# The output product of a decoder layer's last block as a three-term f32r split instead of fp32

## The reference

```
q, k, v = x @ Wq, x @ Wk, x @ Wv                    # heads split
attn = softmax(k . q / sqrt(256)) over the last axis # "bkq"
z = (attn @ v) with heads merged                     # 4096 tokens x 256
z = l2_normalize(z @ Wo)
z = l2_normalize(z @ Wff)
z = gelu(z)                                          # exact gelu
out = layernorm(x + z)
```

## Time and profile before

| | us |
|---|---|
| median of 3 runs | 1932.04 (1929.75 to 1933.5) |
| the profiled execution | 1932.61 |
| its span (first to last instruction) | 1930.8 |
| output stage in it, 1853.3 to the end | 77.5 |

### The profile page before, as it was taken

The page is one execution under the profiler, slowest core; times in us unless marked ns, Lnnn a source line. Parts: engine busy times, 40 slices in busy tenths (PEclk is TensorE's granted clock), DMA queues, the critical chain, the costliest instruction groups (busy, mean ns, idle before and its releaser), DMA issues. The chain is left out here.

```text
span 1930.8 us, 45100 instructions
## 1 busy us (share of the span) xinstructions
PE 1802.6 (93%) x16198; PEld 1200.4 (62%) x16198; DVE 1458.1 (76%) x2707; ACT 1509.4 (78%) x4429; POOL 670.7 (35%) x778
## 2 busy tenths in 40 slices
PE   6999999999999999779999988899999999999995
PEld 5888888888888888648999987722222222222232
DVE  7677777777777777535666665599999999989956
ACT  6777777777777777437898865599999999989964
POOL 2343344433333344303766640022222222222222
PEclk9999999999999999989999998999999999999998
DMA  7233332233323322152101006733453344335002
GB/s 175 45 62 61 61 61 61 62 60 58 63 57 63 62 59 54 23 157 60 33 25 44 18 4 145 232 45 45 63 70 45 52 65 61 45 49 80 6 19 69
DMA packets 139782, 121.74 MB, mean 63 GB/s; under 512 B 78875, under 2 KB 111535, under 8 KB 139567
## 3 DMA queue, kind: packets, MB, share of 16 engines
q1 hardware_dynamic: 139567, 118.88, 31.3%
HBM read 77.29 MB, written 41.53 MB: 62 GB/s over the span
## 5 line engine op out<-in xcount | busy, mean ns | idle before, releaser
L1918 DVE TENSOR_REDUCE s_neg_max<-s_ring 128x1 f32<-128x1024 f32 x512 | 580.7, 1211 | 24.4 <-PE s_ring L1832 24.2
L1880 ACT ACTIVATE s_prob<-s_ring,s_neg_max 128x1024 f32<-128x1024 f32 x512 | 570.5, 1115 | 14.7 <-DVE s_neg_max L1918 14.6
L1845 PE MATMUL s_acc<-s_prob,s_v_norm 128*32 128x256 f32 x4096 | 327.9, 393 | 11.9 <-ACT f_zT_all L1872 9.8
L1832 PE MATMUL s_ring<-f_stack 128*128 128x512 bf16 x1024 | 312.6, 388 | 11.6 <-ACT s_prob L1880 7.0
L1901 POOL TENSOR_TENSOR s_row_inv<-s_row_sum,s_neg_one 128x4 f32<-128x4 f32 x128 | 128.9, 1007 | 411.8 <-ACT s_prob L1880 411.8
L492 ACT ACTIVATE a_prob<-a_psum,a_neg_max 128x128 f32<-128x128 f32 x512 | 179.8, 377 | 60.6 <-DVE a_neg_max L691 60.6
L1845 PEld LDWEIGHTS s_acc<-s_prob,s_v_norm 128*32 128x32 f32 x4096 | 81.5, 108 | 229.7 <-issue 213.3
L586 POOL TENSOR_SCALAR a_relu_ring<-a_qT 128x512 f32<-128x512 f32 x64 | 98.7, 1558 | 343.1 <-ACT a_qT L463 315.8
L1832 PEld LDWEIGHTS s_ring<-f_stack 128*128 128x128 bf16 x1024 | 58.4, 97 | 235.5 <-ACT s_prob L1880 216.2
L731 DVE SCALAR_TENSOR_TENSOR a_att<-a_psum,a_keep_cols,a_num_s 128x128 f32<-128x128 f32 x256 | 72.1, 344 | 132.7 <-ACT a_num_s L514 132.7
L1271 ACT ACTIVATE x_prob<-x_psum,x_neg_max 128x77 f32<-128x77 f32 x512 | 160.8, 337 | 14.2 <-DVE x_neg_max L1428 14.1
(11 more groups left out here) (197 smaller groups left out, 4043.2 us busy)
## 6 DMA issues: line engine op xcount, KB each, us to landing
f_stack<-qk_thirds SPq DMA_DIRECT2D x256, 128.0 KB, 6.0
segment_values<-a_v_stage SPq DMA_DIRECT2D x64, 256.0 KB, 3.5
a_v_pos<-segment_values SPq DMA_DIRECT2D x512, 32.0 KB
qk_thirds<-p_third SPq DMA_DIRECT2D x16, 768.0 KB, 8.0
a_x_in<-in_x_dram SPq DMA_DIRECT2D x16, 256.0 KB, 3.3
a_x_res<-in_x_dram SPq DMA_DIRECT2D x32, 128.0 KB, 2.9
after_attention<-a_normed SPq DMA_DIRECT2D x32, 128.0 KB, 2.4
x_x_in<-after_attention SPq DMA_DIRECT2D x32, 128.0 KB, 2.1
```

Source lines behind the costliest of these rows:

```text
L1832: last = pe.matmul(ring[n % 3][:, f * HALF:(f + 1) * HALF], k_stack[:, slot, j, kt * P:(kt + 1) * P], q_stack[:, slot, j, f * HALF:(f + 1) ...
L1845: last = pe.matmul(acc[32 * j:32 * j + 32, s], v_norm[:, step // KT % 2, step % 4, j, :], prob[:, step % 4, j, s], start=step % (2 * KT) = ...
L1880: act.activation(prob[:, step % 4, j, :], ring[n % 3][:, :], ACT.Exp, bias=neg_max[:, step % 2, j:j + 1], accum_out=row_sum[:, step % 4, j ...
L1918: dve.tensor_reduce(neg_max[:, step % 2, j:j + 1], ring[n % 3][:, :], AX_X, ALU.max, negate=True).then_inc(max_ready, 1)
```

## The change

The product z @ [Wo | Wo Wff] is made from f32r parts by the same `split_matmuls` as the projections. `w_both` becomes `w_split`, a high and a low f32r tensor. Wo is loaded into a tensor of its own, `w_out`; its high part is copied by ScalarE after batch 0 of the thirds and its low part subtracted by GpSimd. Of the folded half the high part is ScalarE's old copy, the low part a new subtraction on VectorE behind it. In the output stage `high(n)` on ScalarE copies a step's z (128x1024 values) to f32r and `low(n)` on VectorE subtracts it from z; both are made two steps ahead, at the head of each iteration, into rings of three slots. TensorE waits for both and issues six f32r matmuls of 512 columns per tile instead of two fp32 ones. GpSimd's order in the output stage is unchanged.

```diff
@@ -1550,10 +1550,10 @@
         stack_landed = [ctx.enter_context(nc.semaphore(f"f_stack{n}_landed")) for n in range(2)]
-        w_both = sb("w_both", [P, ZC, 2 * D])
-        emit_thirds(nc, x2_all, wq, wk, wv, wo, wff, parts, v_all, w_both, stacks, stack_landed, B, S)
+        w_split = [sb(f"w_{part}", [P, ZC, 2 * D], F32R) for part in ("hi", "lo")]
+        emit_thirds(nc, x2_all, wq, wk, wv, wo, wff, parts, v_all, w_split, stacks, stack_landed, B, S)
         zT_all = sb("zT_all", [P, B, ZC, S])
         emit_key_softmax(nc, parts, v_all, stacks, stack_landed, zT_all, B, S)
-        emit_gelu_output(nc, x2_all, zT_all, w_both, out, B, S)
+        emit_gelu_output(nc, x2_all, zT_all, w_split, out, B, S)
 
 
-def emit_thirds(nc, x2_all, wq, wk, wv, wo, wff, parts, v_all, w_both, stacks, stack_landed, B, S):
+def emit_thirds(nc, x2_all, wq, wk, wv, wo, wff, parts, v_all, w_split, stacks, stack_landed, B, S):
 
@@ -1589,2 +1589,4 @@
             sem("both_taken"))
+        wo_high, wo_low, both_low = sem("wo_high"), sem("wo_low"), sem("both_low")
+        w_out = sb("w_out", [P, ZC, D])
         woT = W[0][:, :, :].rearrange("p a b -> p (a b)")
@@ -1607,3 +1609,3 @@
                     at = 32 * j + half * HD
-                    sp.dma_start(w_both[at:at + HD, :, 0:D],
+                    sp.dma_start(w_out[at:at + HD, :, :],
                                  wo.rearrange("(c r h i) n -> r h i c n", c=ZC, r=2, h=4)[half, j]
@@ -1675,3 +1677,3 @@
                         at = (c * ZC + g) * P
-                        last = pe.transpose(wide[0][:, at:at + P], w_both[:, g, c * P:(c + 1) * P], ident[:, :])
+                        last = pe.transpose(wide[0][:, at:at + P], w_out[:, g, c * P:(c + 1) * P], ident[:, :])
                 last.then_inc(wo_turned, 1)
@@ -1725,4 +1727,7 @@
                          ).then_inc(high_done, 1)
-            for b in range(B):
-                batch(b, b % 2, b == 0, b == B - 1)
+            batch(0, 0, True, False)
+            act.wait_ge(wo_landed, 16 * 8)
+            act.copy(w_split[0][:, :, 0:D], w_out[:, :, :]).then_inc(wo_high, 1)
+            for b in range(1, B):
+                batch(b, b % 2, False, b == B - 1)
             act.wait_ge(wo_turned, 1)
@@ -1730,3 +1735,3 @@
             act.wait_ge(both_done, 1)
-            act.copy(w_both[:, :, D:2 * D], wide[1][:, 0:ZC * D].rearrange("p (g n) -> p g n", g=ZC)
+            act.copy(w_split[0][:, :, D:2 * D], wide[1][:, 0:ZC * D].rearrange("p (g n) -> p g n", g=ZC)
                      ).then_inc(both_taken, 1)
@@ -1739,2 +1744,5 @@
                                pattern=[[-1, P]], channel_multiplier=1).then_inc(c_ident, 1)
+            pool.wait_ge(wo_high, 1)
+            pool.tensor_tensor(w_split[1][:, :, 0:D], w_out[:, :, :], w_split[0][:, :, 0:D].bitcast(F32), ALU.subtract
+                               ).then_inc(wo_low, 1)
 
@@ -1777,2 +1785,5 @@
                 batch(b, b % 2, b == B - 1)
+            dve.wait_ge(both_taken, 1)
+            dve.tensor_tensor(w_split[1][:, :, D:2 * D], wide[1][:, 0:ZC * D].rearrange("p (g n) -> p g n", g=ZC),
+                              w_split[0][:, :, D:2 * D].bitcast(F32), ALU.subtract).then_inc(both_low, 1)
 
@@ -1921,3 +1932,3 @@
 
-def emit_gelu_output(nc, x2_all, zT_all, w_both, out, B, S):
+def emit_gelu_output(nc, x2_all, zT_all, w_split, out, B, S):
 
@@ -1935,2 +1946,4 @@
         psum = ctx.enter_context(nc.psum_tensor("g_psum", [P, 2 * GT, 2 * D], F32))
+        zT_hi = sb("zT_hi", [P, 3, ZC, HALF], F32R)
+        zT_lo = sb("zT_lo", [P, 3, ZC, HALF], F32R)
         neg_half = sb("neg_half", [P, 2 * GT])
@@ -1952,3 +1965,3 @@
 
-        c_set = sem("set")
+        c_set, high_ready, low_ready = sem("set"), sem("high_ready"), sem("low_ready")
         z_done, squared, norm_step, clamps_ready, roots_ready, both_ready = (
@@ -1960,2 +1973,6 @@
 
+        def z_part(n):
+            at = n % PER_BATCH * HALF
+            return zT_all[:, n // PER_BATCH, :, at:at + HALF]
+
         block = ctx.enter_context(nc.Block())
@@ -1977,2 +1994,4 @@
             for n in range(STEPS):
+                pe.wait_ge(high_ready, n + 1)
+                pe.wait_ge(low_ready, n + 1)
                 if n >= 2:
@@ -1980,7 +1999,6 @@
                 for t in range(GT):
-                    at = n % PER_BATCH * HALF + t * P
-                    for g in range(ZC):
-                        last = pe.matmul(psum[:, n % 2 * GT + t, :], zT_all[:, n // PER_BATCH, g, at:at + P],
-                                         w_both[:, g, :], start=g == 0, stop=g == ZC - 1)
-                    last.then_inc(z_done, 1)
+                    tokens = slice(t * P, (t + 1) * P)
+                    split_matmuls(pe, psum[:, n % 2 * GT + t, :],
+                                  [(zT_hi[:, n % 3, g, tokens], zT_lo[:, n % 3, g, tokens]) for g in range(ZC)],
+                                  [(w_split[0][:, g, :], w_split[1][:, g, :]) for g in range(ZC)]).then_inc(z_done, 1)
 
@@ -2006,4 +2024,13 @@
 
+            def high(n):
+                if n >= 3:
+                    act.wait_ge(z_done, (n - 2) * GT)
+                act.copy(zT_hi[:, n % 3, :, :], z_part(n)).then_inc(high_ready, 1)
+
+            high(0)
+            high(1)
             squares(0, range(0, 2))
             for n in range(STEPS):
+                if n + 2 < STEPS:
+                    high(n + 2)
                 squares(n, range(2, GT))
@@ -2083,3 +2110,12 @@
 
+            def low(n):
+                dve.wait_ge(high_ready, n + 1)
+                dve.tensor_tensor(zT_lo[:, n % 3, :, :], z_part(n), zT_hi[:, n % 3, :, :].bitcast(F32), ALU.subtract
+                                  ).then_inc(low_ready, 1)
+
+            low(0)
+            low(1)
             for n in range(STEPS):
+                if n + 2 < STEPS:
+                    low(n + 2)
                 clamps(n)
```

## The result

| | before | after |
|---|---|---|
| median of 6 runs beside each other | 1933.41 us (1929.75 to 1934.03) | 1941.28 us (1940.11 to 1942.36) |
| ratio to before | | 1.0044, 95% interval 1.0031 to 1.0057 |
| profiled execution; its span | 1932.61; 1930.8 us | 1941.31; 1939.5 us |

The changed kernel is slower by 7.9 us of median. The ratios of this text are computed over the single runs of a pair, not from the two medians, and differ from the medians' quotient by up to 0.0006. The forecast was 1939.1 (1934.8 to 1943.0), by +7.05 us.

What follows compares the result with a forecast made beforehand. The prediction took a closed ring through gelu, VectorE and GpSimd in the output stage, not TensorE, as the bound. Loop 4.55 + fill 0.2 + clock 1.6 + fold 0.7 = +7.05 us, forecast 1939.1 us, range 1934.8 to 1943.

Steps and rivals of the forecast that it cites:

- The ring: Output stage: gelu, g_y, statistics, g_rstd, g_roots, g_both_inv, gelu set the 7.82 us step; TensorE's shorter burst gains nothing.
- The loop: Output stage steps: VectorE's low(n+2) ahead of the clamps costs 0.91 us in five iterations, +4.55 us.
- two ways to this number: Output stage: late clamps delay g_roots 0.87 to 0.91 us; or g_rstd is held 0.91 by the subtraction's SBUF reads.
- g_roots would be seen released by g_clamped: Sign in the output stage's changed profile: g_roots' wait for g_rstd becomes a wait for g_clamped.
- the sum by the full block: Output stage: g_rstd held for all 1.05 us instead of 0.91 per step, making the sum 0.7 us more.
- The fill: Output stage's start: +0.2 us for preparing and matmuls, +1.6 for 8 matmuls at the low clock (bounds 0 and +3.2).
- The fold: End of the fold's block: a 128x512 subtraction between ScalarE's copy and the next stage, +0.7 us (bounds 0 and 0.9).
- the copy of w_hi behind batch 0: Preparation: falls into 2.65 us in which ScalarE waits for TensorE; cost 0, or up to 1.04.
- (a): Output stage loop: low clock makes bursts 10.2 us and TensorE sets the step, 9 us more, 1948; chance 0.07.
- (b): Output stage loop: the subtraction is covered and costs nothing; 1933 to 1934.5, no measurable change; chance 0.16.
- (c): Output stage loop: TensorE is the bound, so steps fall to about 6.9 us; faster, 1928; chance 0.05.
- (d): Three-term product doesn't reach 0.227 us per matmul; the fill pays 36 times the excess; chance 0.04.

Runs made afterwards that it cites:

- second kernel: Changed kernel with the subtraction low(n+2) moved behind factors(n), where VectorE waits for gelu; 1936.69 us, ratio 1.0017.
- the opened ring: Kernel before, fp32 product kept, only the output stage reordered so gelu(n+1) no longer waits for step n's statistics; 1925.96 us, ratio 0.9952.
- third kernel: Changed kernel with the subtraction low(n+2) directly behind the clamps instead of ahead of them; 1940.22 us, ratio 1.0026.
- fourth kernel: Kernel with low(n+2) behind the factors, plus three extra one-operand BATCH_NORM_STATS2 ahead of the clamps in iterations 1 to 5; 1940.41 us, ratio 1.0029.
- the ten matmuls: Changed kernel plus ten f32r matmuls, results overwritten, ahead of TensorE's first wait in the output stage; 1938.36 us, ratio 1.0017.

## Why the prediction was right

**The ring, not TensorE.** Right. 24 matmuls in place of 16 records shortened each burst and no step by itself; seven steps at 7.82 us with the split in place (second kernel) show that the product's gain was worth nothing, and the opened ring shows where it comes to count.

**The loop, 5 x 0.91 = 4.55.** Measured 5 x 0.905 = 4.5, and the last two steps at 7.81. The prediction had two ways to this number and let the clamps arrive with the hold. VectorE and GpSimd of the kernel after show which came last (timeline):

```profile
1883.69 1.22 DVE L2113 TENSOR_TENSOR g_zT_lo<-f_zT_all,g_zT_hi 128x1024 fp32r<-128x1024 f32 x1
...
1885.42 0.17 DVE L2074 TENSOR_SCALAR g_clamped<-g_scaled 128x4 f32<-128x4 f32 x1
```

```profile
1883.86 1.91 POOL L2054 TENSOR_TENSOR g_rstd<-g_var_eps,g_neg_half 128x4 f32<-128x4 f32 x1 [5.20 <-DVE g_var_eps L2097]
1885.74 1.63 POOL L2048 TENSOR_TENSOR g_roots<-g_clamped,g_neg_half 128x8 f32<-128x8 f32 x1
```

g_clamped is there at 1885.59, with a hand-over of 0.07 at 1885.66; g_rstd ends at 1885.77. So the hold set the step, by about 0.1 us, and by these rows the order alone would have cost about 0.80. The prediction had the two arrive together because it took 0.12 to 0.16 for the hand-over. That the two ways come so close together is luck of the lengths. I wrote that g_roots would be seen released by g_clamped; it follows g_rstd without a wait, and that line of the forecast was wrong. The Trainium skill (SBUF — State Buffer, Who interferes with whom) has the later of two such instructions fully blocked. The overlap here is 1.05 us (1883.86 to 1884.91) and g_rstd is 0.90 us longer, so by this trace it is held for most of the overlap, not all of it. Nor is the later one always held: in the third kernel the subtraction starts beside a running g_rstd and keeps its 1.22. The measurement decides, and the sum by the full block, 0.7 us higher, is not what came.

**The fill, 0.2 + 1.6 for the clock.** Measured +3.09 us to gelu(0) (15.85 against 12.76). Without the low clock it was +0.32, against my 0.2. The clock is the mis-sized term: 2.4 to 2.8 us instead of 1.6. I had counted 8 matmuls at the 1.2 GHz level, from two stretches of 3.4 and 3.6 us. The stretch above shows 14 matmuls in 5.99 us at 0.50, 0.20 us dearer each: 14 x 0.20 = 2.8. For this profile the upper bound that I named, 3.2 after the row of 1695.70, was the nearer one. The 1.6 did come, in two of the six executions with that pause; the other four paid 2.2 to 2.8. So the term is a spread with two ends that the trace of before had both shown, and I had taken the lower for the likely one. One of my two rows for it was also misread. The 3.60 us from 1166.37 are not how long the low level lasted, but what was left of it: the clock had stood at 0.50 since 1156.3, 13.7 us in all, through TensorE's wait (busy times by stretch, kernel before):

```profile
1162.20:1166.30 4.10, 0.00 (x0) 0.00 (x0) 3.03 (x4) 3.48 (x5) 0.00 (x0) 0.50 0.22 58
```

**The fold, 0.7.** Measured 0.74. Before, the next stage began 0.89 us after ScalarE's copy began; now the subtraction stands between (timeline, kernel after):

```profile
1248.87 0.59 ACT L1736 CAST f_w_hi<-p_wide 128x512 fp32r<-128x512 f32 x1 [2.10 <-PE p_wide L1686]
1249.49 0.69 DVE L1787 TENSOR_TENSOR f_w_lo<-p_wide,f_w_hi 128x512 fp32r<-128x512 f32 x1 [5.28 <-ACT f_w_hi L1736]
...
1250.50 0.38 PE L1843 MATMUL s_ring<-f_stack 128*128 128x512 bf16 x1 [1.67 <-PEq L1561]
```

1250.50 - 1248.87 = 1.63 us. Of the 1.3 us of this stage the other 0.57 arise in its first batch, where 12 matmuls came at the low level in this execution against 8 before. The forecast had no term for that; in the profiles of the other kernels with the split this stage is 0.7 to 1.3 us longer than before, so I read it as spread of the clock between executions. From there to the fold ScalarE's rows stand by the same 0.55 to 0.58 us later, so the copy of w_hi behind batch 0 cost nothing, as forecast.

**The rivals.** (a) The low clock came in the loop too, in two of six bursts of the first profile, and no step was longer. The margin was thinner than I had worked out for 3.4 us at 0.50: with 6.8 us at 0.50, in the step above, the burst took 8.6 us instead of 5.7, and ScalarE was through with the squares 0.67 us before it began the gelu. (b) The subtraction covered: out, but true one place further on; it wanted the wait for gelu, where VectorE is idle for 1.6 us. (c) TensorE as the bound: out for this order, and right for the old product once the ring is opened. (d) Out: in the fill of the kernel after, once the clock was at 1.00, the 22 steps from the matmul at 1863.07 to that at 1868.06 are 0.227 us each.

The terms measured give 4.54 + 3.09 + 0.74 = 8.4 us against the forecast's 7.05, and 1.2 of the 1.3 us between them are the clock in the fill. The medians differ by 7.9: part of the closeness to 7.05 is luck, since which clock a median run meets in the fill is open by about 1.2 us. The range's lower end, 1934.8, is 0.7 below what its two terms make (1939.1 - 1.6 - 2 = 1935.5).

## What to carry to other kernels

Before an engine that is 93% busy is made faster, look whether it waits once per step for the same partner. If it does, a closed ring of small instructions sets the step; open the ring by order alone, and only then does the faster product pay. Work that is added to an idle engine costs by its place, not by its length: the same 1.22 us cost 0.91, 0.61 or 0 us per step in three places on the same engine.

## What the runs showed of the hardware

- A GpSimd instruction on 4 or 8 elements per partition was held when it started beside a running VectorE subtraction of two SBUF operands: g_rstd 1.91 us instead of 1.01, and g_roots 2.25 instead of 1.64. Where it had begun first, neither it nor the subtraction (1.22) was longer.
- Beside one-operand BATCH_NORM_STATS2 both kept their time (g_rstd 1.01 in the fourth kernel, g_roots 1.64 with the ring opened). Started after the first of four g_o_fin, which read one large SBUF operand, they did not: g_roots 1.73 to 1.75 in the fourth kernel, g_rstd 1.32 in the opened ring with the old product.
- Around one and the same pause of TensorE, 3.8 us ahead of the output stage, the 0.50 level lasted 3.4, 6.8 or 10.2 us; in the last case (three executions) it had begun 1.4 to 1.8 us before the pause. gelu(0) came at 14.67, 15.85 and 15.26 to 15.47 us by these, at 13.1 with the ten matmuls in the pause.
- With the ring opened, g_rstd lasted 1.98 to 2.13 us in the steps with a subtraction and 1.25 to 1.32 in those without. VectorE and ScalarE do not wait for it in the rows shown, since nothing in the ring waits for g_rstd any more.
